# Quantised feed-forward spread over four slots, residual bias on VectorE, key loads at the head of their slot

## The reference

```python
x = x + _L0_xattn_ref(_layernorm(x), ctx_768, Wq0, Wk0, Wv0, Wo0, bo0)
x = x + _L0_ffn_ref(_layernorm(x), w_gate, w_up, w_down)
x = x + _L1_xattn_ref(_layernorm(x), ctx_768, Wq1, Wk1, Wv1, Wo1, bo1)
x = x + _L1_ffn_ref(_layernorm(x), rhs)

def _L1_ffn_ref(lhs, rhs):
    lhs_scale = _absmax_scale(lhs, (2,))
    rhs_scale = _absmax_scale(rhs, (0,))
    q_lhs = jnp.clip(jnp.round(lhs / lhs_scale), -INT8_MAX, INT8_MAX).astype(jnp.int8)
    ...
    return acc.astype(jnp.float32) * lhs_scale * rhs_scale
```

## Time and profile before

| What | Before |
| --- | --- |
| median of 3 runs (lowest to highest) | 1759.67 us (1755.85 to 1760.43) |
| the profiled execution: its own time / its span | 1758.15 / 1756.4 us |
| PE busy in the span | 1637.0 us, 93% |
| DVE / ACT / POOL busy | 77% / 78% / 72% |
| mean granted PE clock | 0.987 |

### The profile page before, as it was taken

One profiled execution on the slowest core, in us unless ns is written; L12 is line 12 of the kernel. 1 busy time (PEld: TensorE's weight loads), 2 busy tenths in 40 slices (PEclk: granted clock), 3 DMA queues, 4 the chain that ended last, 5 costly groups with the idle time before them and its releaser, 6 DMA issues.

```text
span 1756.4 us, 56619 instructions
## 1 busy us (share of the span) xinstructions
PE 1637.0 (93%) x16300; PEld 1334.3 (76%) x16300; DVE 1355.6 (77%) x3473; ACT 1373.5 (78%) x5650; POOL 1271.7 (72%) x1920
## 2 busy tenths in 40 slices
PE   6999769999999999999999999999899999899995
PEld 3555447888888888888888888777777777777773
DVE  5666647788888888888888877777777777777774
ACT  5565558888888888888888888788888888888883
POOL 3000158888888888887888877788888888888883
PEclk9999989999999999999999999999999999999998
DMA  8677767767666666666666777898888888888893
GB/s 224 226 242 245 257 142 140 135 144 153 139 141 150 142 141 147 142 142 150 144 140 148 146 135 149 153 176 170 172 174 174 178 176 173 175 174 173 179 174 83
DMA packets 807767, 288.45 MB, mean 164 GB/s; under 512 B 686001, under 2 KB 795473, under 8 KB 807697
## 3 DMA queue, kind: packets, MB, share of 16 engines
q1 hardware_dynamic: 806432, 282.87, 73.4%
q0 software_dynamic: 1264, 4.72, 0.9%
HBM read 87.72 MB, written 65.54 MB: 87 GB/s over the span
## 4 chain that ended last, share of the span: by engine, by line
PE 54%; POOL 9%; SPq 8%; issue 8%; DMA 3%; DVE 3%; ACT 1%; POOLq 0%; ACTq 0%; DVEq 0%
PE psum L967 12%; PE psum L980 12%; PE psum L1003 9%; PE psum L957 8%; PE psum L995 6%; SPq L846 5%; PE psum L1010 5%; POOL pr L1433 3%; DMA kb<-keys 2%; POOL p L1439 2%; POOL p L1437 2%; PE psum L943 2%; SPq L830 2%; DVE oT_l L1214 1%; ACT ex L1137 1%
## 5 line engine op out<-in xcount | busy, mean ns | idle before, releaser
L1137 ACT ACTIVATE ex<-psum,nmax 128x77 f32<-128x77 f32 x2048 | 636.6, 332 | 69.2 <-DVE nmax L1288 65.6
L1137 ACT ACTIVATION_READ_ACCUMULATOR ex<-psum,nmax 128x1 f32 x2048 | 435.5, 213 | 0.0
L1439 POOL TENSOR_TENSOR p<-pr,p 128x308 f16<-128x308 f32 x512 | 393.8, 769 | 41.1
L1433 POOL TENSOR_TENSOR pr<-ex,rden 128x308 f32<-128x308 f32 x512 | 359.2, 702 | 40.9 <-DVE rden L1293 37.6
L1288 DVE TENSOR_REDUCE nmax<-psum 128x4 f32<-128x308 f32 x512 | 240.0, 469 | 171.4 <-PE psum L957 165.2
L1437 POOL CAST p<-pr 128x308 f16<-128x308 f32 x512 | 233.4, 456 | 105.8 <-POOL pr L1433 103.4
L980 PE MATMUL psum<-wo_h,oT_h 128*128 128x256 f16 x1024 | 280.6, 274 | 23.5 <-DVE oT_l L1214 22.9
L957 PE MATMUL psum<-kb,qT_h 128*128 128x154 f16 x2048 | 257.9, 231 | 47.9 <-DMA kb<-keys 32.6
L967 PE MATMUL psum<-xT_h,wq_h 128*128 128x256 f16 x1024 | 281.3, 275 | 1.4 <-DVE xT_l L1214 1.4
L967 PE MATMUL psum<-xT_l,wq_h 128*128 128x256 f16 x1024 | 281.4, 275 | 0.0
L967 PE MATMUL psum<-xT_h,wq_l 128*128 128x256 f16 x1024 | 281.4, 275 | 0.0
(11 more groups left out here) (162 smaller groups left out, 3760.0 us busy)
## 6 DMA issues: line engine op xcount, KB each, us to landing
keys<-ks SPq DMA_DIRECT2D x14, 1408.0 KB, 6.3
kb<-keys SPq DMA_DIRECT2D x256, 77.0 KB, 3.2
vb<-vals SPq DMA_DIRECT2D x128, 154.0 KB
vals<-vs SPq DMA_DIRECT2D x56, 256.0 KB, 2.4
x_pair<-in_x_dram SPq DMA_DIRECT2D x32, 256.0 KB, 2.7
pT<-p SPq DMA_TRANSPOSE x512, 3.2
x_res<-in_x_dram SPq DMA_DIRECT2D x32, 256.0 KB, 3.2
mid_x<-y SPq DMA_DIRECT2D x32, 256.0 KB, 2.5
```

The costliest lines, as they stand in the source:

```text
L1137: last = act.activation(ex[i][:, t, b, :], SC[:, t, b * NK:(b + 1) * NK], ACT.Exp, bias=nmax[i][:, t, b:b + 1], accum_out=den[i][:, t, b:b ...
L1433: pool.tensor_tensor(pr[:, t, :, :], ex[i][:, t, :, :], r, ALU.mult).then_inc(s_p, 1)
L1439: pool.tensor_tensor(d[:, t, 1, :, 0:NK], pr[:, t, :, :], d[:, t, 0, :, 0:NK], ALU.subtract).then_inc(s_pl, 1)
```

## The change

- SP: both key loads open their slot, ahead of its transposing transfers; the loads of `x_res` and `xn` go behind both transposing transfers of their slot; the output of a batch is stored in slot 1 of the next body, and the last one behind the loop.
- DVE in layer 1: `spreads` behind `nmax` of slot 0 and `moments` behind `oT_l`; `shift` at the end of slot 0; `am`, `lsc` and `linv` in slot 1, `q_i` in slot 2, `qiT`, `ya` and `yo` in slot 3, with `yo` the last step ahead of `x1`, which now waits for it. DVE adds layer 1's bias in slot 2.
- POOL: `inverse` for layer 1 behind the first `probabilities` of slot 0; no bias in layer 1, and layer 0's in slot 1.
- ACT in layer 1: `normalise` behind all exponentials of slot 0, `q_a` behind those of slot 1.
- PE in layer 1: the transposition of `q_i` at the end of slot 2, `quantised` in slot 3.

```diff
@@ -757,8 +757,6 @@
     if u == 1:
...
-        if lay[-2] == 1:
-            out.append(("turned_q", 0))
...
@@ -767,9 +765,11 @@
     if u == 2:
...
         if lay[-2] == 1:
-            out += [("quant", 0), ("quant", 1)]
+            out.append(("turned_q", 0))
...
+    if u == 3 and lay[-2] == 1:
+        out += [("quant", 0), ("quant", 1)]
...
@@ -872,8 +872,8 @@
-if lay[-2] == 1:
-    b_out = ready(h - 2 - B)
+if lay[-3] == 1:
+    b_out = ready(h - 3 - B)
...
@@ -886,28 +886,17 @@
-    if u == 0 and lay[-1] is not None:
-        after(sp, s_x1, h - 1)
-        if lay[-1] == 1:
-            sp.sem_inc(s_ngo, 1)
-            sp.wait_ge(s_y, 16 * (h - 1 - B + 2))
-        sp.dma_start(x_res[:, :, :], batch_of(x_src[lay[-1]], b_res)).then_inc(s_xr, 16)
+    if u == 0 and lay[0] is not None and like > 0:
+        sp.wait_ge(s_s, QT * n)
+        load_keys(1, at_own, lay[0])
+    if u == 2 and lay[1] is not None:
+        sp.wait_ge(s_s, QT * (n + 2))
+        load_keys(0, at_next, lay[1])
...
-    if u == 2 and lay[2] == 1:
-        sp.wait_ge(s_ys, 16 * (h + 4 - B))
-        sp.sem_inc(s_ngo, 1)
-        sp.wait_ge(s_xt, h + 2)
-        sp.dma_start(xn, batch_of(n_rows, b_far)).then_inc(s_nl, 16)
-    if u == 2 and lay[1] is not None:
-        sp.wait_ge(s_s, QT * (n + 2))
-        load_keys(0, at_next, lay[1])
-    if u == 3 and lay[-2] == 1:
-        sp.wait_ge(s_ysum, h - 1 - B)
-        sp.dma_start(batch_of(out_rows, b_out), yo[:, :, :]).then_inc(s_yo, 16)
...
@@ -916,12 +905,23 @@
+    if u == 1 and lay[-3] == 1:
+        sp.wait_ge(s_ysum, h - 2 - B)
+        sp.dma_start(batch_of(out_rows, b_out), yo[:, :, :]).then_inc(s_yo, 16)
+    if u == 0 and lay[-1] is not None:
+        after(sp, s_x1, h - 1)
+        if lay[-1] == 1:
+            sp.sem_inc(s_ngo, 1)
+            sp.wait_ge(s_y, 16 * (h - 1 - B + 2))
+        sp.dma_start(x_res[:, :, :], batch_of(x_src[lay[-1]], b_res)).then_inc(s_xr, 16)
+    if u == 2 and lay[2] == 1:
+        sp.wait_ge(s_ys, 16 * (h + 4 - B))
+        sp.sem_inc(s_ngo, 1)
+        sp.wait_ge(s_xt, h + 2)
+        sp.dma_start(xn, batch_of(n_rows, b_far)).then_inc(s_nl, 16)
...
-    if u == 0 and lay[0] is not None and like > 0:
-        sp.wait_ge(s_s, QT * n)
-        load_keys(1, at_own, lay[0])
...
@@ -929,6 +929,8 @@
+sp.wait_ge(s_ysum, B)
+sp.dma_start(batch_of(out_rows, B - 1), yo[:, :, :]).then_inc(s_yo, 16)
...
@@ -1066,9 +1068,6 @@
-    if u == 1 and lay[-2] == 1:
-        pe.wait_ge(s_qi, h - 1 - B)
-        turn(as_f16(bank("turned_q", 0)), q_i).then_inc(s_qt, 1)
...
@@ -1076,12 +1075,12 @@
-    if u == 2 and lay[-2] == 1:
+    if u == 3 and lay[-2] == 0:
+        gate_up(3, bank("gu", 3))
+    if u == 3 and lay[-2] == 1:
         pe.wait_ge(s_qe, h - 1 - B)
         for t in range(QT):
             quantised(t, bank("quant", t))
-    if u == 3 and lay[-2] == 0:
-        gate_up(3, bank("gu", 3))
...
@@ -1089,6 +1088,9 @@
+    if u == 2 and lay[-2] == 1:
+        pe.wait_ge(s_qi, h - 1 - B)
+        turn(as_f16(bank("turned_q", 0)), q_i).then_inc(s_qt, 1)
...
@@ -1165,10 +1167,9 @@
-    if u == 0 and lay[-2] is not None:
+    if u == 0 and lay[-2] == 0:
...
-        if lay[-2] == 0 or like == B + 2:
-            after(act, s_xt2, h - 2)
+        after(act, s_xt2, h - 2)
...
@@ -1187,6 +1188,11 @@
     if lay[0] is not None:
         exponentials(n + u, u % 2, 1)
     if u == 0 and lay[-2] == 1:
+        act.wait_ge(s_nmr[1], h - 1)
+        if like == B + 2:
+            after(act, s_xt2, h - 2)
+        normalise(x2, x1, rs2, 1, s_x2)
+    if u == 1 and lay[-2] == 1:
         act.wait_ge(s_li, h - 1 - B)
...
@@ -1293,40 +1299,31 @@
-    if u == 0 and lay[-2] is not None:
+    if u == 0 and lay[-2] == 0:
...
-    if u == 1 and lay[-2] == 1:
-        quantising_scale(h - 2 - B)
...
-    if u == 3 and lay[-2] == 1:
-        for t in range(QT):
-            dve.wait_ge(s_a1, QT * (h - 2 - B) + t + 1)
-            dve.scalar_tensor_tensor(out=ya[:, t, :], in0=bank("quant", t)[:, 0, :],
-                                     scalar=lsc[:, t:t + 1], in1=rhs_sb[:, :], op0=ALU.mult,
-                                     op1=ALU.mult).then_inc(s_ya, 1)
...
-    if u == 3 and lay[-2] == 1:
-        dve.wait_ge(s_ya, QT * (h - 1 - B))
-        after(dve, s_yo, 16 * (h - 2 - B))
-        dve.tensor_tensor(yo[:, :, :], ya[:, :, :], x1[:, :, :], ALU.add).then_inc(s_ysum, 1)
...
-    if u == 0 and lay[-2] is not None:
+    if u == 0 and lay[-2] == 0:
...
+    if u == 0 and lay[-2] == 1:
+        dve.wait_ge(s_x1, h - 1)
+        spreads(x1, st2, s_st2)
...
-    if u == 1 and lay[-2] == 1:
-        dve.wait_ge(s_qa, QT * (h - 1 - B))
-        after(dve, s_qt, h - 2 - B)
-        dve.tensor_scalar(q_i[:, :, :], q_a[:, :, :], MAGIC + INT8_MAX, MAGIC,
-                          ALU.min, ALU.subtract).then_inc(s_qi, 1)
+    if u == 3 and lay[-2] == 1:
+        dve.wait_ge(s_qt, h - 1 - B)
+        after(dve, s_a1, QT * (h - 2 - B))
+        dve.tensor_scalar(qiT[:, :, :], as_f16(bank("turned_q", 0)), -INT8_MAX, None,
+                          ALU.max).then_inc(s_qe, 1)
...
@@ -1338,8 +1335,10 @@
-    if u == 0 and lay[-2] is not None:
+    if u == 0 and lay[-2] == 0:
...
+    if u == 0 and lay[-2] == 1:
+        moments(1, st2, mv2, ve2, s_st2, s_mv2, h - 2)
...
@@ -1350,31 +1349,49 @@
+    if u == 1 and lay[-2] == 1:
+        dve.wait_ge(s_x2, QT * (h - 1))
+        dve.tensor_reduce(am[:, :], x2[:, :, :], AX_X, ALU.max,
+                          apply_absolute_value=True).then_inc(s_am, 1)
+    if u == 2 and lay[-2] == 1:
+        dve.wait_ge(s_qa, QT * (h - 1 - B))
+        after(dve, s_qt, h - 2 - B)
+        dve.tensor_scalar(q_i[:, :, :], q_a[:, :, :], MAGIC + INT8_MAX, MAGIC,
+                          ALU.min, ALU.subtract).then_inc(s_qi, 1)
+    if u == 2 and lay[-1] == 1:
+        dve.wait_ge(s_xr, 16 * h)
+        bias = bo_b[lay[-1]][:, :].unsqueeze(1).to_broadcast([P, QT, D])
+        dve.tensor_tensor(x_res[:, :, :], x_res[:, :, :], bias, ALU.add).then_inc(s_xb, 1)
+    if u == 3 and lay[-2] == 1:
+        for t in range(QT):
+            dve.wait_ge(s_a1, QT * (h - 2 - B) + t + 1)
+            dve.scalar_tensor_tensor(out=ya[:, t, :], in0=bank("quant", t)[:, 0, :],
+                                     scalar=lsc[:, t:t + 1], in1=rhs_sb[:, :], op0=ALU.mult,
+                                     op1=ALU.mult).then_inc(s_ya, 1)
...
-    if u == 1 and lay[-2] == 1:
-        dve.wait_ge(s_qt, h - 1 - B)
-        after(dve, s_a1, QT * (h - 2 - B))
-        dve.tensor_scalar(qiT[:, :, :], as_f16(bank("turned_q", 0)), -INT8_MAX, None,
-                          ALU.max).then_inc(s_qe, 1)
...
+    if u == 1 and lay[-2] == 1:
+        quantising_scale(h - 2 - B)
...
+    if u == 0 and lay[-2] == 1:
+        shift(1, mv2, rs2, h - 1)
+    if u == 3 and lay[-2] == 1:
+        dve.wait_ge(s_ya, QT * (h - 1 - B))
+        after(dve, s_yo, 16 * (h - 2 - B))
+        dve.tensor_tensor(yo[:, :, :], ya[:, :, :], x1[:, :, :], ALU.add).then_inc(s_ysum, 1)
...
-    if u == 0 and lay[-2] == 1:
-        dve.wait_ge(s_x2, QT * (h - 1))
-        dve.tensor_reduce(am[:, :], x2[:, :, :], AX_X, ALU.max,
-                          apply_absolute_value=True).then_inc(s_am, 1)
...
@@ -1391,6 +1408,8 @@
     if u == 3 and lay[-1] is not None:
         dve.wait_ge(s_oa, h)
         dve.wait_ge(s_xb, h)
         after(dve, s_x2, QT * (h - 1))
+        if lay[-2] == 1:
+            dve.wait_ge(s_ysum, h - 1 - B)
...
@@ -1454,19 +1473,21 @@
...
+    if u == 0 and lay[-2] == 1:
+        inverse(1, ve2, rs2, h - 1)
...
-    if u == 0 and lay[-1] is not None:
+    if u == 1 and lay[2] == 0:
+        inverse(0, ve1, rs1, h + 2)
+    if u == 1 and lay[-1] == 0:
         pool.wait_ge(s_xr, 16 * h)
         bias = bo_b[lay[-1]][:, :].unsqueeze(1).to_broadcast([P, QT, D])
         pool.tensor_tensor(x_res[:, :, :], x_res[:, :, :], bias, ALU.add).then_inc(s_xb, 1)
-    if u == 1 and lay[2] == 0:
-        inverse(0, ve1, rs1, h + 2)
...
-    if u == 3 and lay[-1] is not None:
+    if u == 3 and lay[-1] == 0:
...
```

## The result

| What | Before | After |
| --- | --- | --- |
| median (lowest to highest), 4 runs each | 1757.76 us (1753.73 to 1760.43) | 1784.87 us (1781.85 to 1786.4) |
| the profiled execution: own time / span | 1758.15 / 1756.4 us | 1784.02 / 1782.2 us |
| one body of layer 1 (mean of 21) | 20.12 us | 21.18 us |
| one body of layer 0 (mean of 22) | 26.19 us | 26.09 us |

The changed kernel is slower: ratio 1.0154, 95% interval 1.0128 to 1.0181. The forecast was 1768 us with a range up to 1779. The sign was right, the size was three times the 0.5% forecast, and the result lies above the range.

The account below looks back on a forecast made before the run. PE, busy for 93%, was taken as the bound; layer 1's body of 18.30 us plus stalls of 0.74, 0.78 and 0.60 gave 20.42 against 20.12. Over 28 bodies +8.4 us: 1766.6, plus 1.5 for the median: 1768 us, range 1748 to 1779.

Parts of the forecast that it names:

- the 0.93 us from `rs` over `nmr` to the normalisation: Layer 1, slot 0 to slot 1: time from `rs` to the normalisation, 0.93 us, a part of slot 1's forecast stall.
- the bias's "0 on the path": Layer 1: POOL loses 1.27 us a body, DVE's addition in slot 2, taken as 0.85 us, adds 0 on the path.
- Key loads: Layer 1, slot 2: keys issued some 2.7 us sooner, so the 1.33 us stall of the scores goes.
- The loads of rows and the output: 0: SP's queue: these transfers go where a body or several slots lie before their use, so they cost 0.
- Slot 0: 0.74: Layer 1, slot 0: PE's stall ahead of `project`, forecast at 0.74 us instead of 0.40.
- The rival with `yo` held by POOL: End of slot 3: `yo` waits 0.70 us for `pr`, 21.1 us a body, 1788 us; halfway, +0.35, 1778; chance 0.07.
- Slot 1: 0.78: Layer 1, slot 1: PE's stall ahead of `project`, forecast at 0.78 us, from none.
- Slot 2: 0.60: Layer 1, slot 2: PE's stall ahead of `project`, forecast at 0.60 us, from none.
- The sum: Layer 1 body: PE's own 18.30 us plus stalls of 0.74, 0.78 and 0.60 make 20.42 us, against 20.12 before.
- 28 bodies: Layer 1: the new order holds in full for about 28 bodies, each 0.30 us longer, +8.4 us.
- SP as the bound at 19.44: Layer 1, rival: with stalls under 1.1 us together, SP's queue sets 19.44 us a body, -19 us, 1741 us; chance 0.22.

## Why the prediction was right or wrong

Two steps failed, the 0.93 us from `rs` over `nmr` to the normalisation (measured 1.40) and the bias's "0 on the path" (measured 0.23 a body). Together they make 0.74 of the 0.76 us by which the period missed.

*Key loads.* Right. No scores wait for `kb`.

*The loads of rows and the output: 0.* Right for this change, but only together with the bias's move. Alone it costs 3.3 us a body.

*The bias: "0 on the path".* Wrong by 0.23 us a body, some 6 us. I said that DVE has no other long step in slot 2 and that POOL waits for `rden` "in those slots anyway". It doesn't: from 1405.08 to 1412.02 POOL works without a wait, so what the bias takes from it arrives a slot later and meets `yo`. The trace of before already spoke against it: there POOL waits for `rden` for 9.6 us in 520, 0.37 a body. I also sized the addition at 0.85; it is 0.93.

*Slot 0: 0.74.* Measured 0.89, and 0.68 without the bias. The rival with `yo` held by POOL was priced at 0.35 to 0.70 and happened with 0.22. That 0.74 is near 0.68 is in part luck: I took 0.85 for `yo`, which was itself a held length (0.69 alone; in the trace of before `pr` began 0.40 us ahead of it), and let `x` start 0.03 us behind `yo`, where it starts 0.14 behind. The two errors nearly cancel: from `yo` to `x` it is 0.83 without the bias, against my 0.88.

*Slot 1: 0.78.* Measured 1.41. The failing term is "from `rs` over `nmr` to the normalisation it is 0.93". I copied a time between two rows from a place where `nmr` came 0.04 us ahead of POOL's next `pr` to a place where it comes 0.07 us behind it. That is worth 0.49 in the chain and 0.51 a body. The rest, 0.15, stands also with a fast `nmr` (0.93): the way from `rden` to POOL is 0.34 and not 0.25 (1414.99 to 1415.33), and its three steps take 2.20 and not 2.13 (1415.33 to 1417.53).

*Slot 2: 0.60.* Measured 0.56.

*The sum.* 20.42 forecast, plus 0.51 and 0.23, is 21.16; measured is 21.18. With both meetings taken away it is 20.47, by slots that are off by -0.06, +0.15 and -0.04. So the mechanism was right, and two meetings of DVE and POOL were left out of the sum. I had named the rule that makes them, called it contention, and then left it out. I also read the 1039 ns of `p` as a mark of a step with two inputs in SBUF. In the trace of before, the `p` of 1.04 us at 1409.36 stands beside `q_i` (1409.36, 0.43 us), which reads one tile, and ends 0.61 us after it.

*How often it counts.* I took 28 bodies. The 25.8 us of the trace over 1.06 us a body are 24.3.

*SP as the bound at 19.44.* It did not come about here: the stalls are 2.86 us together, and SP waits 37.9 us in 520. Its number is not confirmed either. Where SP's queue does set the pace, in the kernel with its order and the bias, a body takes some 19.55 us, no period is below 19.57, and those of 19.57 and 19.58 were reached with SP waiting from 0.7 to 42.8 us in 520. So SP's waiting time in one trace gave a bound some 0.1 us too low.

*The range.* It ended at 1779 because it left out the upper part of one small rival. The same pair of engines met at a second place that I had not looked for, and the two meetings together are 0.74 us a body.

## What to carry to other kernels

When a step of VectorE with two inputs in SBUF is moved, look at what GpSimd starts within its own length on either side: a 0.16 us step can cost 0.65, and the order of two starts 0.1 us apart decides which engine pays. Lengths taken from a trace may already be held ones, so take the shortest of the same step. If the VectorE step is on the path, holding GpSimd back for it can pay; one wait more gave 0.8% in the changed kernel, and nothing where SyncE's queue was a bound (19.70 and 19.69 us). A cost put on an engine that runs without a wait does not vanish but comes out at its next meeting, and moves of a load and of its consumer are to be priced as a pair.

## What was not expected of the hardware

- A step of 128 x 2 values on VectorE takes 160 to 161 ns alone and 643 to 646 ns when a GpSimd step of 0.70 us started 0.07 us ahead; it ends with it, within 0.02 us. In between it took 432 to 462 ns in the kernel with the early inverse.
- The cost falls on whichever comes second: `pr` takes 0.70 us alone, and 1.14 to 1.22 us where `yo` had begun; a cast of 0.44 us took 0.98 where the bias had begun 0.01 us ahead of it, with the store on ScalarE.
- The held step ends its own length less 0.14 us after the end of the holder (0.13 to 0.15 in 1463 of 1465 cases of six kinds of step in sixteen traces).
- A VectorE step that reads only one tile in SBUF can hold GpSimd as well: `q_i`, 0.42 us, from fp32 to fp16, makes a cast of 0.44 us take 0.62 in the changed kernel, whether the bias is whole or one column. `x`, which reads PSUM and one tile in SBUF, took 690 to 693 ns in layer 1 of every trace.
- The same addition of 128 x 512 values with both inputs in SBUF took 0.68 us undisturbed on VectorE, 0.93 in the changed kernel and 1.25 in the median in the kernel with the bias's move alone; on GpSimd it took 1.27.
- The output's store, and then the load of the rows too, could be moved from SyncE's to ScalarE's queue with the period at 19.58, 19.57 and 19.58 us.
